# Scores ahead of the query projection, norm logarithm ahead of the query squares, in a pipelined windowed-attention kernel

## The chip, the cores and the metric

One core of one Trainium2 chip runs the whole program. The metric is the time of one execution on the device, in microseconds (us). The core's engines work side by side and meet at semaphores: TensorE (PE in the rows, its weight loads PEld), VectorE (DVE), ScalarE (ACT), GpSimd (POOL) and SyncE (SP), which issues the transfers.

## What is computed

x is 8 sequences of 256 tokens of 128 numbers. After a layer norm one branch is a linear attention with a small convolution; the other is six layers, each a windowed attention and a gated feed-forward part. The result is x plus the first branch times silu of the second. Nearly all of the time goes to the six layers:

```python
def attn_layer(x, Wqkv, qs, ksc, Wo):
    q, k, v = split(x @ Wqkv)             # 16 heads of 64
    q = l2norm(q) * qs;  k = l2norm(k) * ksc
    q, k = rotary(q), rotary(k)
    out = local_attention(q, k, v)        # window 32: own window and the one before
    return out @ Wo

for i in range(6):
    x = attn_layer(shift_tokens(x), ...) + x
    x = ffn_layer(shift_tokens(x), ...) + x
```

## The kernel before

**Units and slots.** A layer of one sequence is a batch: 6 layers x 8 sequences are 48 batches, numbered n. A batch has four units u = 4n + j, j = 0 to 3: two groups of eight heads by two tiles of 128 tokens. The program is software-pipelined by hand. Each engine runs a loop over n, and its body writes out four slots, j = 0 to 3; a slot does the projections of unit u and later steps of older units. The order inside a slot is the order of the code, engine by engine, and engines wait for each other by counting semaphores. The first five batches and the last one are written out, the rest are loops with the same body.

**TensorE's slot** (body, L791): the query projection of unit u (project, L661: three matmuls of 512 columns, high and low parts of the numbers); the scores of unit u-3 (scores, L675: 64 matmuls of 64 columns into ps_s); the turned probabilities of u-4 (turn_p, L652); the key and value projections of u; q and k of u-2 turned into ps_s (turn_qk, L639); work of the feed-forward part and the output projection, which differs by slot; the values of u-4 (L701); at the end of slot 0 ln_spread (L741).

**ScalarE's slot** (body, L1066): copy of the attention output of u-5 (keep_attention, L1007), copy of v of u-1 (keep_v, L962), squares of the query projection of u (squares_of, L955), logarithm and exponential that give a first value of the norms of u-1 (start_norms, L1000), in slot 2 a square for the layer norm, the turned probabilities of u-4 (keep_p, L988: two copies), the exponential of the softmax of u-3 (L996), squares of the key projection, the copies of the turned q and k of u-2, the mask for the scores of u-2, which is copied into ps_s (lay_mask, L974), and in slots 1 to 3 two feed-forward copies. In slot 0 it ends with the table load for the gelu and the gelu itself; in slot 1 the table with logarithm and exponential is loaded again (load_exp, L1063), between the squares and start_norms.

**VectorE's slot** (body, L1373): steps of the layer norm and the feed-forward part in slots 1 to 3, the maximum and the shift of the softmax of u-3 (softmax_shift, L1298: row_max, then prob), the Newton steps of the norms of u-1 (newton, L1286: rn_a, rn_b, rnorm), the sums of the query squares of u (L1273), the rotary step on q of u (rotate, L1255: qk and qk_rot), the row sums of the softmax of u-3 (L1309), the rotary step on k, the sums of the key squares, and the clamp of the sums (L1278: ssq_c).

**GpSimd's slot** (body, L475): one of the gate of the feed-forward part (slot 1), the split of a slice of the next layer's weights (slot 2, not in the last layer) and the rounding of the next x (slot 3); then it multiplies q and k of u-1 with the norms, divides the probabilities of u-3 (L440) and adds the two halves of the rotary step of u.

**Who waits for whom, around the change.** The query projection of u waits for the rotary step on q of u-1, which frees ps_q; in slot 0 it also waits for the rounded x and the split weights. The scores of u-3 wait for q_turned, k_turned and mask_laid, which ScalarE gives at the end of the slot before. The squares of u wait for the query projection of u. start_norms of u-1 waits for the clamp of u-1, which is the last step of VectorE's slot before. The Newton step of u-1 waits for start_norms. The turning of q and k of u-2 waits for the softmax shift of u-3, since both use ps_s. The turned probabilities wait for the copy of the attention output of u-5.

Of the kernel before, what the change touches and what calls it, by code (L numbers as in the profile page):

```python
# [62 lines left out]
def build(nc, x, wq, wk, wv, wp, bp, conv_w, conv_b, wqkv, q_scale, k_scale, wo, ln_g, ln_b, w1, b1, w2,  # L63
          rotary, masks, eye, head_block, out):
    with ExitStack() as ctx:
# [9 lines left out]
        def sem(name):  # L75
            return ctx.enter_context(nc.semaphore(name))
# [77 lines left out]
        ps_q, ps_k, ps_qs, ps_tk = ps_qk[:, 0, :], ps_qk[:, 1, :], ps_s[:, 0, :], ps_s[:, 1, :]  # L154
# [3 lines left out]
        def scored(pair):  # L158
# [27 lines left out]
        q_done, k_done, v_done = sem("q_done"), sem("k_done"), sem("v_done")  # L186
# [10 lines left out]
        q_scaled, k_scaled, ssq_done, ssq_clamped, rn_step, rnorm_done = (  # L197
            sem(n) for n in ("q_scaled", "k_scaled", "ssq_done", "ssq_clamped", "rn_step", "rnorm_done"))
# [7 lines left out]
        def live(u):  # L206

            return not isinstance(u, int) or 0 <= u < UNITS * STEPS

        def live_batch(m):  # L210
            return not isinstance(m, int) or 0 <= m < STEPS

        def place(n, j, back):

            return n + (j - back) // UNITS, (j - back) % UNITS

        def wait(eng, s, value):

            if not isinstance(value, int) or value > 0:
                eng.wait_ge(s, value)  # L220
# [316 lines left out]
        def _(pe):  # L537
# [123 lines left out]
            def project(n, j, i, ps, free, done):  # L661

                u = UNITS * n + j
                octet, tile = j // 2, j % 2
                if j == 0 and i == 0:
                    pe.wait_ge(xs_ready, n + 1)
                    pe.wait_ge(w_split, n // BATCHES * SLICES + SLICES)
                wait(pe, free, u)
                toks = slice(P * tile, P * tile + P)
                cols = span(n // BATCHES % 2 * (3 * INNER) + i * INNER + octet * OCTET, OCTET)  # L670
                mm(ps[:], xs_hi[:, toks], w_hi[:, cols], True, False)
                mm(ps[:], xs_hi[:, toks], w_lo[:, cols], False, False)
                mm(ps[:], xs_lo[:, toks], w_hi[:, cols], False, True).then_inc(done, 1)

            def scores(u, j, s, pair=ps_s, laid=True):  # L675

                octet, tile = j // 2, j % 2
                pe.wait_ge(q_turned, u + 1)
                pe.wait_ge(k_turned, u + 1)
                if laid:  # L680
                    pe.wait_ge(mask_laid, u + 1)
                    nc.tensor.sem_inc(pe_passed, 1)
                else:
                    for head in range(2):
                        mm(pair[:, head, 0:OCTET // 2], ident_b[:], mask_b[:, tile, OCTET // 2 * head:OCTET // 2 * (head + 1)],
                           True, True)
                for g in range(4):
                    for odd in range(2):
                        w = 2 * (g % 2) + odd
                        for low in range(2):  # L690
                            c = 2 * (g // 2) + low
                            at = 64 * odd + WINDOW * low
                            for head in range(2):
                                rows = slice(64 * head, 64 * head + 64)
                                last = mm(pair[at:at + WINDOW, head, 64 * g:64 * g + 64],
                                          q_t[rows, s, P * c + WINDOW * w:P * c + WINDOW * w + WINDOW],
                                          k_t[rows, octet, c, WINDOW * (4 * tile + w):WINDOW * (4 * tile + w) + 64],
                                          False, True, skip_group_check=True)
                last.then_inc(s_done, 1)
# [91 lines left out]
            def body(n):  # L791
                for j in range(UNITS):
                    u = UNITS * n + j
                    project(n, j, 0, ps_q, q_scaled, q_done)
                    if live(u - 3):
                        scores(u - 3, (j - 3) % UNITS, (j - 3) % 2)
                    if live(u - 4):
                        turn_p(u - 4, j % 2)
                    project(n, j, 1, ps_k, k_scaled, k_done)
                    if isinstance(n, int) and u == 0:  # L800
                        bias_fold()
                    project(n, j, 2, ps_v, v_copied, v_done)
                    if live(u - 2):
                        turn_qk(u - 2, 0, j % 2)
                        turn_qk(u - 2, 1, j % 2)
                    if j == 0:
                        if live_batch(n - 5):
                            ff_down(n - 5)
                        if live_batch(n - 2):
                            out_projection(n - 2, 1)  # L810
                    if j == 1:
                        if live_batch(n - 2):
                            ln_mean(n - 2)
                        if live_batch(n - 3):
                            ff_up(n - 3, 0)
                    if j == 2:
                        if live_batch(n - 2):
                            ln_variance(n - 2)
                        if live_batch(n - 3):
                            ff_up(n - 3, 1)  # L820
                    if j == 3:
                        if live_batch(n - 3):
                            ff_up(n - 3, 2)
                        if live_batch(n - 1):
                            out_projection(n - 1, 0)
                    if live(u - 4):
                        values(u - 4, n - 1, j, j % 2)
                    if j == 0 and live_batch(n - 3):
                        ln_spread(n - 3, u, BATCHES + n - 4)
# [55 lines left out]
        def _(act):  # L885
# [69 lines left out]
            def squares_of(u, i, s):  # L955

                wait(act, ssq_done, 2 * (u - 2) + i + 1)
                act.wait_ge((q_done, k_done)[i], u + 1)
                nc.scalar.activation(squares[:, s, OCTET * i:OCTET * i + OCTET], (ps_q, ps_k)[i][:], ACT.Square  # L959
                                     ).then_inc((q_squared, k_squared)[i], 1)  # L960

            def keep_v(u, n, j):  # L962
                wait(act, o_done, u - 3)
                if j % 2 == 0:
                    wait(act, v_shifted[j + 1], 32 * n)
                act.wait_ge(v_done, u + 1)
                copy(v_own[:, j, :], ps_v[:]).then_inc(v_copied, 1)
# [32 lines left out]
            def start_norms(c, s):  # L1000

                act.wait_ge(ssq_clamped, c + 1)
                nc.scalar.activation(ssq_ln[:, s, :], ssq_c[:, s, :], ACT.Ln).then_inc(ssq_logged, 1)
                act.wait_ge(ssq_logged, c + 1)
                nc.scalar.activation(rn_0[:, s, :], ssq_ln[:, s, :], ACT.Exp, scale=-0.5).then_inc(rn_started, 1)
# [60 lines left out]
            def body(n):  # L1066
                for j in range(UNITS):
                    u = UNITS * n + j
                    if live(u - 5):
                        keep_attention(u - 5, *place(n, j, 5))  # L1070
                    if live(u - 1):
                        keep_v(u - 1, *place(n, j, 1))
                    squares_of(u, 0, j % 2)
                    if j == 1 and live_batch(n - 4):
                        load_exp()
                    if live(u - 1):
                        start_norms(u - 1, (j - 1) % 2)
                    if j == 2 and live_batch(n - 2):
                        ln_square(n - 2)
                    if live(u - 4):  # L1080
                        keep_p(u - 4, j % 2)
                    if live(u - 3):
                        softmax_exp(u - 3, (j - 3) % 2)
                    squares_of(u, 1, j % 2)
                    if live(u - 2):
                        keep_turned_q(u - 2, j % 2)
                        keep_turned_k(u - 2, (j - 2) % UNITS)
                        lay_mask(u - 2, j % 2)
                    if j >= 1 and live_batch(n - 3):
                        ff_copy(n - 3, j - 1)  # L1090
                    if j == 0 and live_batch(n - 4):
                        load_gelu()
                        gelu(n - 4)
                    if j >= 1 and isinstance(n, int) and n == LAST:
                        silu_start(j - 1)
# [421 lines left out]
```

## Time and profile before

| | us |
|---|---|
| median of 3 runs | 1680.26 |
| lowest, highest | 1675.05, 1681.73 |
| profiled execution, its own time | 1673.91 |
| its span | 1672.1 |

| engine | busy us | share of the span |
|---|---|---|
| TensorE matmul | 1592.4 | 95% |
| VectorE | 1474.8 | 88% |
| ScalarE | 1433.8 | 86% |
| GpSimd | 1314.5 | 79% |

The profile covers one execution. Its timeline rows are: start, duration, engine, line of the kernel, operation, what is written <- what is read, shape, count, and in brackets the idle time of the engine before it with what ended that. Matmuls overlap in the pipeline, so the start of the next one tells more than the end of one. Small VectorE and ScalarE operations overlap their neighbours by a tenth of a microsecond in the same way. The mean granted clock of TensorE over the execution is 0.987 of full speed.

### The profile page before, as it was taken

The page shows a single profiled execution, that of the slowest core. Times are in us where ns is not written, and L with a number is a line of the kernel's source. Part 1 is how long each engine was busy: PE and PEld are TensorE (multiplying, and loading weights), DVE is VectorE, ACT ScalarE, POOL GpSimd, SP SyncE. Part 2 cuts the span into 40 slices and gives each one's busy share as a digit, 9 for nine tenths or more (in the row PEclk, how much of TensorE's full clock was granted, in tenths as well). Part 3 has the DMA queues.
Part 4 walks back from the last instruction along what each step waited for, and adds up shares of the span by engine and source line. Part 5 has one row for each costly group of instructions (what it writes and reads, how often), then busy time and mean ns, then how long its engine had stood idle before and what let it go on. Part 6 is the DMA issues. An engine that isn't in the chain of part 4 may idle for free.

```text
span 1672.1 us, 69023 instructions
## 1 busy us (share of the span) xinstructions
PE 1592.4 (95%) x25972; PEld 1222.7 (73%) x25972; DVE 1474.8 (88%) x3011; ACT 1433.8 (86%) x2851; POOL 1314.5 (79%) x1305
## 2 busy tenths in 40 slices
PE   7779999999999999999999999999999999999995
PEld 5657777777777777777777777777777777777773
DVE  4499999999999999999999999999999999999974
ACT  4267998998899899889989989998998999999985
POOL 6088888888888888888878888887888878777865
PEclk9799999999999999999999999999999999999998
DMA  4111111111111111111111111111111101111000
GB/s 135 48 43 40 34 40 38 32 45 31 46 40 33 38 38 39 40 43 37 31 38 44 41 37 40 35 31 50 40 38 34 39 28 39 37 31 34 29 25 26
DMA packets 41426, 66.40 MB, mean 40 GB/s; under 512 B 7072, under 2 KB 16032, under 8 KB 41376
## 3 DMA queue, kind: packets, MB, share of 16 engines
q1 hardware_dynamic: 40224, 65.38, 13.1%
q8 instruction: 33, 0.54, 0.1%
q10 hardware_dynamic: 1152, 0.34, 0.1%
q14 instruction: 17, 0.14, 0.0%
HBM read 20.61 MB, written 1.05 MB: 13 GB/s over the span
## 4 chain that ended last, share of the span: by engine, by line
PE 58%; DVE 26%; issue 12%; ACT 3%; DVEq 1%; DMA 0%; POOL 0%; ACTq 0%; POOLq 0%
PE ps_s L539 13%; PE ps_a L539 11%; PE ps_qk L539 10%; PE ps_f L539 9%; PE ps_po L539 7%; DVE qk_rot L1269 5%; PE ps_v L539 4%; DVE qk L1267 4%; PE ps_po L658 4%; DVE ssq L1275 4%; DVE row_sum L1311 3%; DVE row_max L1302 3%; DVE prob L1305 2%; DVE xc L1324 1%; DVE rn_b L1292 1%
## 5 line engine op out<-in xcount | busy, mean ns | idle before, releaser
L436 POOL TENSOR_TENSOR qk<-qk,rnorm 128x512 f32<-128x512 f32 x384 | 393.4, 1046 | 142.7 <-DVE rnorm L1295 134.0
L428 POOL TENSOR_TENSOR qk<-qk,qk_rot 128x512 f32<-128x512 f32 x384 | 484.8, 1285 | 0.0
L443 POOL TENSOR_TENSOR prob<-prob,row_inv 128x512 f32<-128x512 f32 x192 | 200.7, 1045 | 115.5 <-DVE row_inv L1314 115.5
L1275 DVE TENSOR_REDUCE ssq<-squares 128x8 f32<-128x512 f32 x384 | 260.4, 678 | 3.4 <-ACT squares L959 3.4
L1267 DVE TENSOR_TENSOR qk<-ps_qk,table 128x512 f32<-128x512 f32 x384 | 262.2, 683 | 1.1
L1269 DVE TENSOR_TENSOR qk_rot<-ps_qk,table 128x512 f32<-128x512 f32 x384 | 260.7, 679 | 0.0
L959 ACT ACTIVATE squares<-ps_qk 128x512 f32<-128x512 f32 x384 | 232.3, 605 | 19.8 <-PE ps_qk L539 12.9
L953 ACT COPY p_bd<-ps_po 64x512 f32<-64x512 f32 x378 | 217.4, 575 | 20.9 <-PE ps_po L658 18.6
L539 PEld LDWEIGHTS ps_s<-ident,qk 128*128 128x128 f32 x1528 | 170.9, 140 | 77.2 <-DVE prob L1305 63.6
L539 PE MATMUL ps_s<-ident,qk 128*128 128x128 f32 x1528 | 202.9, 276 | 23.8 <-DVE prob L1305 22.9
L539 PE MATMUL ps_qk<-w_hi,xs_hi 128*128 (+1 forms) x384 | 189.1, 493 | 11.4 <-DVE qk_rot L1269 6.7
L539 PEld LDWEIGHTS ps_po<-p_bd,v_back 128*64 128x64 f32 x3056 | 162.2, 137 | 45.4 <-issue 31.4
L539 PE MATMUL ps_po<-p_bd,v_back 128*64 128x64 f32 x3056 | 192.9, 225 | 0.0
L539 PE MATMUL ps_po<-p_bd,v_own 128*64 128x64 f32 x3056 | 188.5, 222 | 0.0
L539 PE MATMUL ps_a<-attn_t,wo_sb 128*64 128x257 f32 x1536 | 185.8, 383 | 0.0
L1302 DVE TENSOR_REDUCE row_max<-ps_s 128x8 f32<-128x512 f32 x191 | 130.6, 684 | 62.5 <-PE ps_s L539 62.3
L539 PEld LDWEIGHTS ps_s<-k_t,q_t 64*32 64x32 f32 x12224 | 133.2, 105 | 70.3 <-issue 70.3
L953 ACT COPY attn_t<-ps_po 128x512 f32<-128x512 f32 x191 | 112.6, 589 | 64.8 <-PE ps_po L539 64.8
L539 PE MATMUL ps_s<-k_t,q_t 64*32 64x64 f32 x12224 | 164.1, 224 | 0.7 <-ACT ps_s L953 0.5
L539 PEld LDWEIGHTS ps_po<-p_bd,v_own 128*64 128x64 f32 x3056 | 155.2, 138 | 0.0
L539 PEld LDWEIGHTS ps_a<-attn_t,wo_sb 128*64 128x64 f32 x1536 | 105.7, 136 | 66.5 <-issue 17.6
L539 PE MATMUL ps_qk<-w_lo,xs_hi 128*128 (+1 forms) x384 | 152.7, 398 | 0.0
(207 smaller groups left out, 3516.9 us busy)
## 6 DMA issues: line engine op xcount, KB each, us to landing
v_back<-v_own SPq DMA_DIRECT2D x192, 192.0 KB, 2.4
w_raw<-in_wqkv SPq DMA_DIRECT2D x48, 192.0 KB, 2.4
v_back<-v_own SPq DMA_DIRECT2D x96, 64.0 KB, 2.1
wo_sb<-in_wo SPq DMA_DIRECT2D x12, 256.0 KB, 3.0
w_sb<-in_w SPq DMA_DIRECT2D x6, 341.0 KB, 3.1
w_sb<-in_w SPq DMA_DIRECT2D x6, 192.0 KB, 2.5
x_in<-in_x SPq DMA_DIRECT2D x4, 256.0 KB, 4.8
out<-s_out SPq DMA_DIRECT2D x8, 128.0 KB, 1.9
```

Source lines behind the costliest of these rows:

```text
L428: nc.gpsimd.tensor_tensor(qk[:, s, i, :], qk[:, s, i, :], qk_rot[:, s, i, :], ALU.add).then_inc(added, 1)
L436: nc.gpsimd.tensor_tensor(heads(qk[:, s, i, :]), heads(qk[:, s, i, :]), rnorm[:, s, 8 * i:8 * i + 8].unsqueeze(2).to_broadcast([P, 8, HEAD ...
L443: nc.gpsimd.tensor_tensor(heads(prob[:, s, :]), heads(prob[:, s, :]), row_inv[:, s, :].unsqueeze(2).to_broadcast([P, 8, HEAD]), ALU.mult). ...
L539: return nc.tensor.matmul(o, lhs, rhs, start=start, stop=stop, **kw)
L658: last = nc.tensor.transpose(ps[:, P * c:P * c + P], prob[:, s, P * c:P * c + P], ident[:])
L953: return nc.scalar.copy(o, i)
L959: nc.scalar.activation(squares[:, s, OCTET * i:OCTET * i + OCTET], (ps_q, ps_k)[i][:], ACT.Square).then_inc((q_squared, k_squared)[i], 1)
L1267: V.tensor_tensor(heads(qk[:, s, i, :]), heads(ps[:]), cos.unsqueeze(1).to_broadcast([P, 8, HEAD]), ALU.mult)
L1269: V.tensor_tensor(halves(qk_rot[:, s, i, :]), halves(ps[:])[:, :, ::-1, :], sin.rearrange("p (a c) -> p a c", a=2).unsqueeze(1).to_broadca ...
L1275: V.tensor_reduce(ssq[:, s, 8 * i:8 * i + 8], heads(squares[:, s, OCTET * i:OCTET * i + OCTET]), AX, ALU.add).then_inc(ssq_done, 1)
L1302: V.tensor_reduce(most, score, AX, ALU.max).then_inc(max_done, 1)
L1311: V.tensor_reduce(row_sum[:, s, :], heads(prob[:, s, :]), AX, ALU.add).then_inc(sum_done, 1)
```

## The change

Two lines move. In TensorE's body the scores of unit u-3 come first in each slot and the query projection of unit u follows. In ScalarE's body start_norms (logarithm and exponential) comes ahead of the query squares in slots 0, 2 and 3; in slot 1, where the table is loaded between the two, it stays behind.

```diff
@@ -791,9 +791,9 @@
             def body(n):
                 for j in range(UNITS):
                     u = UNITS * n + j
-                    project(n, j, 0, ps_q, q_scaled, q_done)
                     if live(u - 3):
                         scores(u - 3, (j - 3) % UNITS, (j - 3) % 2)
+                    project(n, j, 0, ps_q, q_scaled, q_done)
                     if live(u - 4):
                         turn_p(u - 4, j % 2)
                     project(n, j, 1, ps_k, k_scaled, k_done)
@@ -1070,10 +1070,12 @@
                         keep_attention(u - 5, *place(n, j, 5))
                     if live(u - 1):
                         keep_v(u - 1, *place(n, j, 1))
+                    if j != 1 and live(u - 1):
+                        start_norms(u - 1, (j - 1) % 2)
                     squares_of(u, 0, j % 2)
                     if j == 1 and live_batch(n - 4):
                         load_exp()
-                    if live(u - 1):
+                    if j == 1 and live(u - 1):
                         start_norms(u - 1, (j - 1) % 2)
                     if j == 2 and live_batch(n - 2):
                         ln_square(n - 2)
```

## Rows read from the trace of the kernel before

**Rows 1.** Windows by slot, batch 23: busy time and count of each engine.
```profile
core 0: us, PE busy (x) PEld busy (x) DVE busy (x) ACT busy (x) POOL busy (x), PEclk, DMA share, GB/s
806.17:815.32 9.15, 9.15 (x150) 7.04 (x150) 8.01 (x17) 8.31 (x15) 6.95 (x7) 1.00 0.17 50
815.32:822.23 6.91, 6.91 (x126) 5.57 (x124) 5.68 (x13) 6.50 (x13) 5.16 (x6) 1.00 0.10 28
822.23:829.48 7.25, 7.23 (x130) 5.59 (x126) 7.11 (x14) 7.07 (x16) 6.84 (x7) 1.00 0.12 36
829.48:838.65 9.17, 8.53 (x140) 6.16 (x138) 8.96 (x20) 7.41 (x18) 7.76 (x9) 1.00 0.07 21
sum 32.48, PE 31.81 PEld 24.37 DVE 29.77 ACT 29.29 POOL 26.71; mean PE 7.95 PEld 6.09 DVE 7.44 ACT 7.32 POOL 6.68
```

**Rows 2.** The same windows for batch 42, in the last layer: their sum.
```profile
sum 31.70, PE 31.57 PEld 24.41 DVE 28.99 ACT 29.16 POOL 25.17; mean PE 7.89 PEld 6.10 DVE 7.25 ACT 7.29 POOL 6.29
```

**Rows 3.** Waits from 200 to 1370 us: who for whom, us, times, longest.
```profile
PEld ps_s L539 <- DVE prob L1305: 51.5, 72, 1.0
DVE row_max L1302 <- PE ps_s L539: 51.2, 72, 0.8
```

**Rows 4.** Timeline, TensorE, head of slot 1: start, us, operation [idle before].
```profile
815.32 0.48 PE L539 MATMUL ps_qk<-w_hi,xs_hi 128*128 x1
...
816.20 0.86 PE L539 MATMUL ps_s<-k_t,q_t 64*32 64x64 f32 x64
816.99 0.66 PE L658 MATMUL ps_po<-ident,prob 128*128 128x128 f32 x4
```

**Rows 5.** Timeline, ScalarE, slot 1.
```profile
816.31 0.60 ACT L959 ACTIVATE squares<-ps_qk 128x512 f32<-128x512 f32 x1 [0.21 <-PE ps_qk L539]
...
818.47 0.22 ACT L1005 ACTIVATE rn<-ssq_ln 128x18 f32<-128x18 f32 x1
```

**Rows 6.** Timeline, VectorE, slot 1.
```profile
817.17 0.69 DVE L1302 TENSOR_REDUCE row_max<-ps_s 128x8 f32<-128x512 f32 x1 [0.82 <-PE ps_s L539]
817.99 0.69 DVE L1305 TENSOR_TENSOR prob<-ps_s,row_max 128x512 f32<-128x512 f32 x1
818.72 0.18 DVE L1289 SCALAR_TENSOR_TENSOR rn_a<-ssq_c,rn 128x18 f32<-128x18 f32 x1
```

**Rows 7.** Timeline, TensorE and VectorE, the turning in slots 2 and 3.
```profile
825.64 0.40 PE L539 MATMUL ps_v<-w_hi,xs_lo 128*128 x1
826.06 0.66 PE L539 MATMUL ps_s<-ident,qk 128*128 128x128 f32 x4
...
833.02 0.69 DVE L1305 TENSOR_TENSOR prob<-ps_s,row_max 128x512 f32<-128x512 f32 x1
833.77 1.09 PE L539 MATMUL ps_s<-ident,qk 128*128 128x128 f32 x8 [0.54 <-DVE prob L1305]
```

**Rows 8.** Timeline, VectorE and TensorE, slot 3 of batch 42.
```profile
1447.50 0.69 DVE L1305 TENSOR_TENSOR prob<-ps_s,row_max 128x512 f32<-128x512 f32 x1
1448.33 1.04 PE L539 MATMUL ps_s<-ident,qk 128*128 128x128 f32 x8
```

**Rows 9.** Timeline, ScalarE's mask in slot 1, TensorE's head of slot 2.
```profile
822.08 0.59 ACT L953 CAST ps_s<-mask_b 128x512 f32<-128x512 bf16 x1
822.23 0.50 PE L539 MATMUL ps_qk<-w_hi,xs_hi 128*128 x1
```

**Rows 10.** Timeline, ScalarE's waits in slot 0 (first row) and slot 3.
```profile
806.11 0.59 ACT L953 COPY attn_t<-ps_po 128x512 f32<-128x512 f32 x1 [1.01 <-PE ps_po L539]
...
832.37 0.22 ACT L1003 ACTIVATE ssq_ln<-ssq_c 128x18 f32<-128x18 f32 x1 [0.58 <-DVE ssq_c L1280]
```

**Rows 11.** A window of the prologue; timeline, one shape at two clocks.
```profile
50.00:60.00 10.00, 6.08 (x42) 4.96 (x42) 5.22 (x10) 4.00 (x7) 0.00 (x0) 1.00 0.01 3
...
1639.76 1.91 PE L539 MATMUL ps_s<-xn,w_sb 128*128 128x256 f32 x4
1655.91 1.03 PE L539 MATMUL ps_s<-xn,w_sb 128*128 128x256 f32 x4
```

## The prediction

> **What bounds the kernel now.** I read the windows by slot first. The span is a pipeline of 48 batches of four slots; from batch 4 on a batch repeats with a period of 32.48 us [rows 1] and, in the last layer, of 31.70 us [rows 2]. The 1170 us that the waits of rows 3 cover hold 36 long periods (a wait that comes twice a batch is counted 72 times there), and the last layer has 8 batches: 44 batches on which a change in the loop acts. In rows 1 TensorE is busy 9.15 of 9.15, 6.91 of 6.91, 7.23 of 7.25 and 8.53 of 9.17 us in slots 0 to 3. VectorE is the fuller one where TensorE isn't: 7.11 of 7.25 and 8.96 of 9.17 us in slots 2 and 3. So neither engine alone is the bound; the bound runs back and forth.
>
> Next the waits [rows 3]. TensorE waits for VectorE's softmax shift (DVE prob) twice a batch, and VectorE waits for the scores (PE ps_s) twice a batch. The timelines place them. In slot 1 TensorE starts the query projection at 815.32, the scores at 816.20, and the next step at 816.99 [rows 4]. ScalarE waits 0.21 us for that projection, then does squares, table load and logarithm, and the exponential starts at 818.47 and takes 0.22 [rows 5]. VectorE waits for the scores until 817.17, starts the shift at 817.99 and the first Newton step at 818.72 [rows 6]. The shift ends at 818.68 and the exponential at 818.69: two paths that both start at the head of slot 1 arrive within 0.01 us, and this is what the forecast turns on. From there VectorE runs on to the shift of slot 3, which ends at 833.71, and TensorE's turning of q and k starts at 833.77 after 0.54 us of idling [rows 7]. Then TensorE has hardly a gap until the head of the next slot 1. The cycle is: TensorE from slot 3 through slot 0 to the head of slot 1; query projection and scores; VectorE through slots 1, 2 and 3; TensorE again. In the last layer the turning of slot 3 starts at 1448.33, after a shift that starts at 1447.50 and ends at 1448.19 [rows 8]: there TensorE itself is last, by about 0.1 us.
>
> **The scores go first.** No instruction is added or removed on TensorE: 64 score matmuls and 3 projection matmuls trade places, as long together as before. The scores come one projection sooner, 816.20 - 815.32 = 0.88 us, and the projection comes one score block later, 816.99 - 816.20 = 0.79 us [rows 4]. What this does in each slot:
>
> Slot 0: VectorE may start its maximum up to 0.88 us sooner. TensorE is full here and doesn't wait for VectorE, so the gain ends in idle time. ScalarE's squares come 0.79 later; behind them it waited for the turned probabilities anyway. Cost: zero, and the cover is TensorE's own queue.
>
> Slot 1, where ScalarE's order isn't changed: the squares start when the later projection is done, 816.31 + 0.79 = 817.10. Queued behind them on ScalarE are the table load, the logarithm and the exponential, which VectorE's Newton step waits for. It starts at 818.72 + 0.79 = 819.51. The shift, for its part, is over 0.88 us sooner, near 817.8, so VectorE stands idle for 1.7 us and everything behind the Newton step is 0.79 late: the sooner scores are worth nothing, because the other of the two equal paths has grown.
>
> Slot 2: the scores now stand at the head, and they need the mask that ScalarE lays at 822.08 to 822.67 in slot 1, while TensorE is free at 822.23 [rows 9]. Until now the query projection filled that time. ScalarE has no wait in which to recover from the head of slot 1 on, so the mask is down at 822.67 + 0.79 = 823.46, the scores start near 823.50, and TensorE idles 1.27 us. From the head of the slot to the turning TensorE took 826.06 - 822.23 = 3.83 us; the last projection before it starts at 825.64 and leaves room after 0.23, at 825.87 [rows 7], so 0.19 of it is waiting and 3.64 is work. It turns at 823.50 + 3.64 = 827.14, 1.08 us late. VectorE is 0.79 late and no longer last.
>
> Slot 3: TensorE was free at 833.77 - 0.54 = 833.23 [rows 7] and is now free at 834.31; VectorE's shift ends at 833.71 + 0.79 = 834.50. VectorE is last, the slot is 0.79 late, and that goes once around the cycle. In the last layer TensorE is last, so the 1.08 of slot 2 stays.
>
> **The norm logarithm goes ahead of the squares** in slots 0, 2 and 3. It is two instructions of 0.22 us [rows 5], the same number as before. In slot 3 ScalarE waited 0.58 us for VectorE's clamped sums after the squares were done [rows 10]; now the squares stand behind that wait, so their start-to-start time of 0.5 us is no longer hidden in it and ScalarE's later work is another 0.5 late, 1.3 in all. It has 1.01 us of waiting before its first copy of the next slot 0 [rows 10], and TensorE's 0.79 on top: 1.3 fits into 1.8. Slot 0 has cover too; in slot 2 the clamped sums are due when ScalarE comes to them, to within 0.1. Cost zero, gain zero: in these slots VectorE never waits for the exponential.
>
> No DMA is issued in another place, SyncE's and GpSimd's queues keep their order, and GpSimd's work follows VectorE's.
>
> **Sum.** 36 x 0.79 = 28.4 us, 8 x 1.08 = 8.6 us, together 37.0 us against the profiled execution's own 1673.9, or 1710.9. That execution is 6.3 us under the median of the runs shown, 1680.3, and a little under their lowest; the sum is added to the median: 1717.3, given as 1717. What the trace doesn't show is how fast a score block starts behind values, and a projection behind scores. The nearest rows: a neighbour pair costs 0.88 for three projection matmuls against 0.79 for the scores [rows 4], so a seam may be worth 0.1 either way, and the four seams of a batch 0.4 either way; 44 x 0.4 = 18 us. I take zero, since each kind of block is still preceded by another one, and keep 18 us on both sides: 1699 to 1735.
>
> **Rivals.** (1) Faster: the sooner scores do pull VectorE ahead. For it: VectorE's two waits for scores are its only regular ones [rows 3]. It would need the Newton step of slot 1 to start before 818.72, that is a table load that isn't held by the squares; against it stand 0.21 us of waiting right ahead of those squares [rows 5]. Then the late mask of slot 2 costs 822.70 - 822.23 = 0.47 less the 0.19 waited there before, 0.28, and the 0.54 waited in slot 3 comes off at best: 36 x 0.54 - 8 x 0.28 = 17 us, 1663.
>
> (2) No change: the change doesn't do what it says. The scores stand first but wait for the mask, the projection waits behind them, and the log's move ahead gives ScalarE back what the squares lose. Some 0.1 us a batch either way, 1676 to 1684.
>
> (3) ScalarE becomes the bound. It is already without a wait from slot 1 to slot 3. If its lateness in slot 3 goes past the 1.8 us worked out above (1.3 by my reckoning), the mask of slot 3 holds the scores at the head of slot 0, and TensorE has nothing to catch up with. With 0.5 us more a batch: 44 x 0.5 = 22 on top, 1739.
>
> (4) TensorE's clock falls in the new 1.27 us gap. The granted clock stays at 1.00 (2.4 GHz) in all four slots with the present gap [rows 1], and even in a stretch in which TensorE was busy 6.08 of 10 us [rows 11]. Where it did fall, four matmuls of 256 columns took 1.91 instead of 1.03 us [rows 11]; 0.85 of some 7 us of one slot is 6 us a batch, 44 x 6 = 264, 1981.
> The Trainium skill (TensorE: Matmul & The Clock Gate, Part 1: The HAM clock gate) says that the clock is not a fixed one: the half rate is the default, and it is the engine's recent activity that releases it. By that rule a change that opens a gap in every batch could cost this; the rows above show no fall after longer pauses of work than this one, and nothing in the forecast rests on the rule.
>
> **How the numbers follow.** Forecast 0.72, faster 0.09, no change 0.10, ScalarE as the bound 0.08, clock 0.01. The likeliest case gives 1717. The range must leave out no more than 0.2: the faster and the no-change case are left out below and the clock above, ScalarE's is taken in, which gives 1694 (5 us of spread between runs below 1699) to 1743. A measurement of this kernel can tell 0.5%, 8.4 us, from no change. Faster by more 0.09, within 0.10, slower 0.81.
>
> **What the profile after would show.** Right: rn_a of slot 1 starts straight behind the exponential, with 1 us or more of VectorE idling; ScalarE waits about 1 us for the query projection ahead of the squares of slot 1, in place of 0.21; TensorE idles about 1.3 us at the head of slot 2, until ScalarE's mask; VectorE's waits for scores are gone or short; the period is 33.3 us (32.8 in the last layer). Wrong: if the first Newton step of slot 1 doesn't come later against the head of the slot, or if ScalarE has a wait somewhere in slots 1 and 2, the sum has no ground; a period of 32.0 us or less would be rival 1, one of 33.8 or more rival 3.

## The result and the profile after

The changed kernel takes 1721.2 us (median of 4 runs, 1717.5 to 1726.4) against 1677.7 us of the kernel before in runs beside it (1673.5 to 1681.7): a ratio of 1.0267, 95% interval 1.0238 to 1.0296. The forecast was slower, 1717 us, 1694 to 1743. The profiled execution has a span of 1720.3 us, 48.2 more than before.

The page's line of busy times, then the window of one long batch, from the head of slot 1 to the head of the next slot 1, which answers to the sum in [rows 1]:

```profile
PE 1573.0 (91%) x25972; PEld 1252.4 (73%) x25972; DVE 1452.7 (84%) x3011; ACT 1437.9 (84%) x2851; POOL 1314.1 (76%) x1305
...
801.22:834.65 33.43, 31.27 (x535) 24.91 (x534) 29.36 (x62) 29.36 (x59) 26.70 (x27) 1.00 0.11 33
```

TensorE's share falls from 95 to 91%, with the same 25972 matmuls and a granted clock of 1.00 in the window. The batch takes 33.43 us where it took 32.48. In the last layer the table load of ScalarE in slot 1 comes once a batch. The pair below (start, duration) is 32.97 us apart, the longest of the six such distances there; their mean is 32.92, where the period was 31.70 [rows 2]:

```profile
1470.88 1.28 ACT L1064 ACT_TABLE_LOAD   x1
...
1503.85 1.28 ACT L1064 ACT_TABLE_LOAD   x1
```

The waits from 200 to 1400 us, which hold the long batches (who for whom, us in total, times, longest), to be held against [rows 3]:

```profile
DVE rn_a L1291 <- ACT rn L1005: 64.2, 36, 1.8
ACT squares L959 <- PE ps_qk L539: 60.4, 71, 1.2
PE ps_s L539 <- ACT ps_s L953: 56.1, 36, 1.6
DVE qk L1269 <- PE ps_s L539: 35.4, 36, 1.0
...
PEld ps_s L539 <- DVE prob L1307: 24.4, 36, 0.7
```

Three waits are new or much longer: VectorE's Newton step for ScalarE's exponential (36 times, 1.8 us each), ScalarE's squares for the query projection, and TensorE's scores for ScalarE's mask (36 times, 1.56 us). VectorE's 51.2 us of waiting for scores [rows 3] are gone from the list; in its place stands a wait of 0.98 us for the turned q in slot 0, where VectorE has time. TensorE's waits for the shift are left in one slot of four instead of two.

Slot 1 of one batch, TensorE, ScalarE and VectorE, against [rows 4 to 6]:

```profile
800.58 0.71 PE L539 MATMUL ps_f<-ident,rnorm 128*128 128x128 f32 x4
801.22 0.86 PE L539 MATMUL ps_s<-k_t,q_t 64*32 64x64 f32 x64
802.01 0.50 PE L539 MATMUL ps_qk<-w_hi,xs_hi 128*128 x1
802.80 0.60 PE L658 MATMUL ps_po<-ident,prob 128*128 128x128 f32 x4
...
803.00 0.60 ACT L959 ACTIVATE squares<-ps_qk 128x512 f32<-128x512 f32 x1 [1.18 <-PE ps_qk L539]
803.62 1.28 ACT L1064 ACT_TABLE_LOAD   x1
805.16 0.22 ACT L1005 ACTIVATE rn<-ssq_ln 128x18 f32<-128x18 f32 x1
...
802.93 0.69 DVE L1307 TENSOR_TENSOR prob<-ps_s,row_max 128x512 f32<-128x512 f32 x1
805.41 0.18 DVE L1291 SCALAR_TENSOR_TENSOR rn_a<-ssq_c,rn 128x18 f32<-128x18 f32 x1 [1.79 <-ACT rn L1005]
```

And the start of ln_spread in the kernel before:

```profile
814.85 0.71 PE L539 MATMUL ps_f<-ident,rnorm 128*128 128x128 f32 x4
```

Counted from the start of ln_spread, the shift starts at 2.35 where it started at 3.14, so the scores did bring it forward by 0.79. The squares start at 2.42 instead of 1.46, the exponential at 4.58 instead of 3.62, and the Newton step at 4.83 instead of 3.87: all three 0.96 later. VectorE's next step in the order of its code is the Newton step, so it idles until then. From the start of this Newton step to the start of the shift of slot 3 it takes 14.32 us (805.41 to 819.73) where it took 14.30 (818.72 to 833.02), in both kernels without a wait: the 0.96 us go through to slot 3, and the mask isn't on that way.

Slots 2 and 3 of the same batch, against [rows 7, 9, 10]: ScalarE's mask, TensorE's scores at the head of slot 2, the turning in slots 2 and 3, ScalarE's logarithm of slot 3 and its first copy of slot 0.

```profile
808.77 0.59 ACT L953 CAST ps_s<-mask_b 128x512 f32<-128x512 bf16 x1
809.61 0.85 PE L539 MATMUL ps_s<-k_t,q_t 64*32 64x64 f32 x64 [1.55 <-ACT ps_s L953]
813.03 1.03 PE L539 MATMUL ps_s<-ident,qk 128*128 128x128 f32 x8
...
820.47 1.09 PE L539 MATMUL ps_s<-ident,qk 128*128 128x128 f32 x8 [0.24 <-DVE prob L1307]
819.07 0.22 ACT L1003 ACTIVATE ssq_ln<-ssq_c 128x18 f32<-128x18 f32 x1 [0.94 <-DVE ssq_c L1282]
825.29 0.59 ACT L953 COPY attn_t<-ps_po 128x512 f32<-128x512 f32 x1 [0.48 <-PE ps_po L539]
```

The turning of slot 2 stands 12.45 us behind ln_spread, against 826.06 - 814.85 = 11.21 before, so 1.24 late; that of slot 3 19.89 against 18.92, so 0.97 late, held by VectorE's shift. TensorE reaches it late in slot 2 and waits for VectorE in slot 3, as worked out.

### The profile page after: what moved, and what is told of

It is laid out like the page before. It is cut to its first block, busy times and chain, and to the rows that moved or that the text cites. A ratio compares the mean times of both kernels' runs of the same rounds, so it can differ in the third digit from the quotient of the medians.

```text
span 1720.3 us, 69023 instructions
## 1 busy us (share of the span) xinstructions
PE 1573.0 (91%) x25972; PEld 1252.4 (73%) x25972; DVE 1452.7 (84%) x3011; ACT 1437.9 (84%) x2851; POOL 1314.1 (76%) x1305
## 4 chain that ended last, share of the span: by engine, by line
PE 53%; DVE 26%; issue 12%; ACT 8%; DVEq 1%; DMA 0%; POOL 0%; ACTq 0%; POOLq 0%
PE ps_s L539 12%; PE ps_a L539 11%; PE ps_qk L539 9%; PE ps_f L539 9%; PE ps_po L539 6%; DVE qk_rot L1271 5%; DVE qk L1269 4%; DVE ssq L1277 4%; PE ps_v L539 3%; DVE row_sum L1313 3%; DVE row_max L1304 3%; ACT L1064 3%; DVE prob L1307 2%; PE ps_po L658 2%; ACT squares L959 2%
## 5 line engine op out<-in xcount | busy, mean ns | idle before, releaser
L539 PEld LDWEIGHTS ps_s<-ident,qk 128*128 128x128 f32 x1528 | 175.1, 140 | 50.0 <-DVE prob L1307 29.6
L539 PE MATMUL ps_qk<-w_hi,xs_lo 128*128 (+1 forms) x384 | 152.5, 397 | 0.0
L539 PE MATMUL ps_f<-xn,w_sb 128*128 128x256 f32 (+1 forms) x556 | 147.5, 388 | 0.5 <-ACT qk_rot L1036 0.5
```

Source lines behind the costliest of these rows:

```text
L539: return nc.tensor.matmul(o, lhs, rhs, start=start, stop=stop, **kw)
```

## The experiments

Theory A is that of the forecast: the loss enters through slot 1, by query projection, squares, table load, logarithm, exponential and Newton step. Theory B, the rival: it is TensorE's idling at the heads of slots 2 and 3, where the scores wait for the mask. Each ratio is to the kernel before, in runs beside it (medians 1676.0 to 1677.4 us).

### Slot 1 alone taken back

```diff
+                    if j == 1:
+                        project(n, j, 0, ps_q, q_scaled, q_done)
                     if live(u - 3):
                         scores(u - 3, (j - 3) % UNITS, (j - 3) % 2)
-                    project(n, j, 0, ps_q, q_scaled, q_done)
+                    if j != 1:
+                        project(n, j, 0, ps_q, q_scaled, q_done)
```

> The changed kernel, but in slot 1 TensorE does the query projection ahead of the scores again. Theory A (the loss enters through slot 1: query projection, squares, table load, logarithm, exponential, Newton step): the 0.95 us a batch go; ScalarE's wait ahead of the squares of slot 1 is 0.2 us again, Newton starts behind the shift, period 32.5 us; in the last layer some 0.3 us a batch stay, since the scores of slot 2 still wait for the mask. Ratio to before 1.000 to 1.003, about 1680 us. Theory B (the loss is TensorE's idling at the head of slot 2, where the scores wait for the mask): the head of slot 2 still idles about 0.5 us of the 1.55 us, so about a third of the 44 us stays: 1692 us or more, ratio 1.009.

Measured: 1677.6 us, ratio 1.0003 (0.9985 to 1.0021). Its waits over the long batches:

```profile
ACT squares L962 <- PE ps_qk L539: 26.9, 72, 0.6
PE ps_s L539 <- ACT ps_s L956: 23.8, 37, 1.4
```

Its table loads in slot 1, from 190 to 1600 us (how many, duration in ns, start of the first and the last):

```profile
L1067 ACT ACT_TABLE_LOAD  x44: 1283/1283/1283, 201.8 to 1593.7; - x44
```

TensorE still waits some 0.65 us a batch for the mask, and the Newton step's wait isn't among the waits any more. The first and the last table load of the loop are 1391.9 us apart, against 1390.2 in the kernel before and 1433.1 in the changed one. In the long batches the loads are 32.47 us apart, as before, so there the mask's wait costs nothing. In the last layer, where TensorE is last, they are 31.97 apart and not 31.70: there it costs 0.27 us a batch, 2 us in all, as the expectation had it, and too little for the ratio to tell. With three of four slots changed and the log ahead, all but these 2 us of the loss are gone. That is theory A, and B's 1692 falls; what is true of B is confined to the last layer.

### Slot 1 alone changed

The kernel before, with `if j == 1` in place of `if j != 1` around the later projection, and ScalarE's order of before.

> The kernel before, but in slot 1 alone TensorE does the scores ahead of the query projection; ScalarE's order is that of before. Theory A: the whole loss is there, 44 x 0.96 = 42 us, 1720 us, ratio 1.025, with 1.8 us of VectorE's waiting ahead of the Newton step of slot 1. Theory B: the heads of slots 2 and 3 do not wait for a mask, so 1680 us, ratio 1.002 or less.

Measured: 1716.7 us, ratio 1.0239 (1.0209 to 1.0269).

```profile
DVE rn_a L1292 <- ACT rn L1008: 64.3, 36, 1.8
...
PE ps_s L539 <- ACT ps_s L956: 24.0, 36, 0.7
...
804.36 0.18 DVE L1292 SCALAR_TENSOR_TENSOR rn_a<-ssq_c,rn 128x18 f32<-128x18 f32 x1 [1.80 <-ACT rn L1008]
```

One slot of four gives the Newton step's wait to the tenth (64.3 against 64.2 us) and nearly the whole loss: 39 of 44 us by the medians, and 41.7 of the 42.9 us by which the stretch between the loop's first and last table load grows. The rest lies in the last layer, where the batch takes 32.66 us here and 32.92 in the changed kernel. The expectation for theory B had no mask wait here; there is one, of 0.67 us behind the projection in slot 2, since the mask itself is late. So this run alone doesn't clear the mask, but it shows where its lateness begins; the run ahead of it and the one without the mask's waits, below, clear it for the long batches.

### One part at a time

ScalarE's part alone (start_norms ahead in slots 0, 2 and 3, TensorE as before):

> Only ScalarE's part of the change: logarithm and exponential ahead of the squares in slots 0, 2 and 3, TensorE's order as before. Forecast of the sum: nothing, ratio 1.000, 0.998 to 1.002. In slot 3 ScalarE's later work comes some 0.5 us later and its wait ahead of the first copy of slot 0 is that much shorter. Rival: the 0.5 us reach the bound in each batch, 44 x 0.5 = 22 us, ratio 1.013.

Measured: 1676.7 us, ratio 0.9998 (0.9986 to 1.0011). The two waits that the sum spoke of, in the kernel before and in this one:

```profile
ACT attn_t L953 <- PE ps_po L539: 44.1, 72, 1.0
...
ACT ssq_ln L1003 <- DVE ssq_c L1280: 20.7, 36, 0.6
```
```profile
ACT ssq_ln L1003 <- DVE ssq_c L1282: 41.6, 71, 1.0
ACT attn_t L953 <- PE ps_po L539: 24.9, 72, 0.5
```

The wait for the clamped sums grows by 20.9 us and the wait ahead of the first copy shrinks by 19.2: the 0.5 us a batch moved from one cover into the other, as the sum had it.

TensorE's part alone (the scores ahead in all slots, ScalarE as before):

> Only TensorE's part of the change: scores ahead of the query projection in all four slots, ScalarE's order as before. Theory A (all of the loss comes through slot 1, where ScalarE's order is the same in both kernels): as slow as the changed kernel, ratio 1.024 to 1.028, about 1720 us; the logarithm's new place is worth nothing here too. Rival: the logarithm ahead of the squares makes up for part of the later squares in slots 0, 2 and 3, where without it the Newton step is held as well: then 1735 us or more.

Measured: 1716.7 us, ratio 1.0246 (1.0226 to 1.0265). Its Newton steps wait in a second slot too, and still it isn't slower:

```profile
DVE rn_a L1289 <- ACT rn L1005: 79.0, 70, 1.8
```

79.0 us in 70 waits against 64.2 in 36: 15 us of waiting more, at no cost in the long batches (33.37 us each, against 33.41 in the changed kernel), because it lies in slot 0, where VectorE has time. In the last layer the batch takes 33.20 us against 32.92, so there the log's new place is worth 0.28 us a batch, 2 us in all; in the long ones it costs 0.04. In sum the whole loss is TensorE's part, and the log's new place neither helps nor hurts with it by the time (the intervals of this and the changed kernel overlap).

### The path dosed without touching TensorE

```diff
+                    if j == 1 and live_batch(n - 4):
+                        act.wait_ge(q_done, u + 1)
+                        wait(act, extra_done, n - 4)
+                        nc.scalar.activation(extra[:], ps_q[:], ACT.Square).then_inc(extra_done, 1)
                     squares_of(u, 0, j % 2)
```

> The kernel before with one more ScalarE operation of 0.49 us (a second square of the same bank into a buffer that nobody reads) ahead of the squares of slot 1, in the 44 batches with a table load. It doses the path squares, table load, logarithm, exponential, Newton step without touching TensorE. Theory A: that path ties with the scores' path to within 0.01 us, so the dose comes out nearly whole: 44 x 0.48 = 21 us, 1698 us, ratio 1.0125. Theory B (ScalarE has room there and the loss of the change is TensorE's): less than 0.1 us a batch, ratio 1.002 or less.

Measured: 1702.7 us, ratio 1.0148 (1.0125 to 1.0170), or 25 us by the ratio, 21 to 28 by its interval. ScalarE's slot 1:

```profile
800.18 0.59 ACT L955 COPY v_own<-ps_v 128x512 f32<-128x512 f32 x1
801.06 0.60 ACT L1078 ACTIVATE extra<-ps_qk 128x512 f32<-128x512 f32 x1 [0.28 <-PE ps_qk L541]
801.55 0.59 ACT L961 ACTIVATE squares<-ps_qk 128x512 f32<-128x512 f32 x1
```

and the copy of v in slot 1 of the kernel before:

```profile
815.51 0.59 ACT L953 COPY v_own<-ps_v 128x512 f32<-128x512 f32 x1
```

From the copy of v to the first square it is 0.88 us, where it was 816.31 - 815.51 = 0.80 [rows 5], then 0.49 more for the extra one: the dose is 0.57, not 0.49, and 44 x 0.57 = 25.1 us. It comes out whole: a long batch takes 33.06 us in this trace where it took 32.47, 0.59 more. The path through the squares has no slack in the kernel before, as [rows 5, 6] said, and a delay on it is paid in full.

### The cure: the table load ahead of the squares as well

```diff
-                    if j != 1 and live(u - 1):
+                    if j == 1 and live_batch(n - 4):
+                        load_exp()
+                    if live(u - 1):
                         start_norms(u - 1, (j - 1) % 2)
                     squares_of(u, 0, j % 2)
-                    if j == 1 and live_batch(n - 4):
-                        load_exp()
-                    if j == 1 and live(u - 1):
-                        start_norms(u - 1, (j - 1) % 2)
```

> The changed kernel, and ScalarE also does the table load, the logarithm and the exponential ahead of the squares in slot 1, so that nothing which the Newton step waits for stands behind the query projection. Theory A: the loss goes, and the sooner scores are worth something for the first time; the Newton step starts behind the shift, about 0.8 us sooner against the head of slot 1 than in the kernel before, but the rotary step of slot 1 then waits for the turned q on TensorE, which leaves 0.2 us a batch: 36 x 0.2 = 7 us, 1670 us, ratio 0.996 (0.993 to 0.999). Theory B: the mask still comes behind the head of slot 2 and TensorE still idles there, 1700 us or more.

Measured: 1666.1 us, ratio 0.9927 (0.9906 to 0.9948). One table load's place turns a loss of 2.7% into a gain of 0.7%. VectorE in slot 1, ln_spread of this batch starting at 808.25:

```profile
810.60 0.69 DVE L1305 TENSOR_TENSOR prob<-ps_s,row_max 128x512 f32<-128x512 f32 x1
811.31 0.34 DVE L1289 SCALAR_TENSOR_TENSOR rn_a<-ssq_c,rn 128x18 f32<-128x18 f32 x1
...
813.07 0.69 DVE L1267 TENSOR_TENSOR qk<-ps_qk,table 128x512 f32<-128x512 f32 x1 [0.38 <-PE ps_s L539]
...
DVE qk L1267 <- PE ps_s L539: 48.5, 72, 1.0
PE ps_s L539 <- ACT ps_s L953: 23.1, 73, 1.3
```

The Newton step starts 3.06 behind ln_spread, 0.81 sooner than before, and the rotary step then waits 0.38 us for the turned q, as expected. The period is 32.23 us (TensorE's query projections of slot 0 at 800.52 and 832.75): 36 x 0.25 = 9 us. In the last layer the batch takes 31.81 us instead of 31.70, so that the whole stretch between the loop's first and last table load is 7.5 us shorter (1382.7 against 1390.2), which is what was expected. The medians differ by 11.3. In the trace the first table load stands at 197.3 us, 3.0 sooner than before, but it also stands 2.2 and 2.7 us sooner in the traces of the two parts of the change alone, which are not faster. So where the rest of the 11 us comes from stays open.

Now without the mask's waits at the heads of slots 2 and 3, where the projection is first again:

> As the kernel with the table load ahead of the squares in slot 1, but in slots 2 and 3 TensorE does the query projection first again, so that the scores there don't wait for the mask at the head (0.3 us of TensorE's idling in each of these slots). Theory A: these waits cost nothing in 36 of 44 batches, since VectorE is last in slots 2 and 3, held by the turned q of slot 1; in the last layer 0.3 us a batch come off: 2 to 3 us, 1664 us, ratio 0.992. Rival: the mask waits hold the cycle, 44 x 0.3 = 13 us come off, 1653 us.

Measured: 1667.4 us, ratio 0.9949 (0.9931 to 0.9967): no gain by the time, whose interval can't tell the 2 to 3 us expected. The same view of the table loads, in the kernel above and in this one:

```profile
L1064 ACT ACT_TABLE_LOAD  x44: 1283/1283/1283, 197.3 to 1580.0; - x44
L1067 ACT ACT_TABLE_LOAD  x44: 1283/1283/1283, 200.8 to 1580.9; - x44
```

The stretch is 2.6 us shorter, 1380.1 for 1382.7, and all of it comes off in the last layer (31.47 us a batch for 31.81). The long batches take 32.23 us in both. That is the clearest blow to theory B: in the 36 batches where VectorE is last its wait can be there or not. In the last layer, where TensorE is last, it costs 0.3 us a batch.

And, added to this last version, a step against the wait that does hold, the one for the turned q:

```diff
+                    if j != 1:
+                        project(n, j, 2, ps_v, v_copied, v_done)
                     if live(u - 2):
                         turn_qk(u - 2, 0, j % 2)
                         turn_qk(u - 2, 1, j % 2)
+                    if j == 1:
+                        project(n, j, 2, ps_v, v_copied, v_done)
```

> As the kernel with slots 0 and 1 swapped and the table load ahead, and in slot 1 TensorE turns q and k of the older unit ahead of the value projection (0.70 us sooner). VectorE's 0.38 us of waiting for the turned q in slot 1 is what holds the cycle now; it goes, and the shift of slot 3 comes that much sooner, until TensorE is last: 36 x 0.38 = 14 us off, 1651 us, ratio 0.984; in the last layer TensorE is last and nothing comes off. If the turned q doesn't hold the cycle, the time stays at that of the kernel without this step.

Measured: 1649.6 us, ratio 0.9846 (0.9829 to 0.9863), the best version here, 27 us under the kernel before.

```profile
805.99 1.03 PE L539 MATMUL ps_s<-ident,qk 128*128 128x128 f32 x8
806.78 0.48 PE L539 MATMUL ps_v<-w_hi,xs_hi 128*128 x1
...
805.68 0.35 DVE L1295 SCALAR_TENSOR_TENSOR rn_a<-ssq_c,rn 128x18 f32<-128x18 f32 x1
806.98 0.68 DVE L1273 TENSOR_TENSOR qk<-ps_qk,table 128x512 f32<-128x512 f32 x1
...
802.63:834.39 31.76, 31.38 (x537) 24.70 (x534) 29.52 (x62) 29.20 (x59) 26.71 (x27) 1.00 0.12 35
```

The turning now starts 3.36 us behind ln_spread (802.63) in place of 4.04 before, VectorE's rotary step follows its sums without a wait, and the batch takes 31.76 us, of which TensorE is busy 31.38. As long as TensorE's work takes these 31.38 us, another order has at most the other 0.4 us a batch to give.

### Is any of it the scores' place?

The table load ahead with TensorE's old order:

> TensorE's order as in the kernel before; on ScalarE, in slot 1 alone, table load, logarithm and exponential ahead of the squares. Theory A (two tied paths): the path through the squares gets 0.8 us shorter, but the path scores, maximum, shift is unchanged and takes over 0.1 us sooner: at most 44 x 0.1 = 4 us off, ratio 0.997 to 1.000. Rival (the logarithm alone is the bound of slot 1, and the gain of 10 us of the kernel that also has the scores first is owed to this step): 1667 us, ratio 0.993.

Measured: 1670.2 us, ratio 0.9965 (0.9950 to 0.9980). 6 us off where at most 4 were expected; the bound lies inside the interval. VectorE in slot 1:

```profile
815.04 0.69 DVE L1307 TENSOR_TENSOR prob<-ps_s,row_max 128x512 f32<-128x512 f32 x1
815.65 0.17 DVE L1291 SCALAR_TENSOR_TENSOR rn_a<-ssq_c,rn 128x18 f32<-128x18 f32 x1
```

The Newton step starts 0.61 us behind the start of the shift, where it started 0.73 behind it in the kernel before (817.99 to 818.72 [rows 6]). Freed of the exponential it overlaps the end of the shift. So the two paths of slot 1 were not equal to 0.01 us: the one through the squares was last, by 0.12. The long batch takes 32.34 us instead of 32.47, and 44 x 0.12 = 5.3 us is the gain.

The same with the turned q ahead too:

> As the kernel with the turned q and k ahead of the value projection in slot 1 and the table load ahead, but with the query projection ahead of the scores in all four slots, as in the kernel before. It asks what the sooner scores are worth in the best version (1650 us). Theory A: the shift path holds slot 1 again, so nearly all of the gain goes: 1672 us, ratio 0.996 (0.994 to 1.000). Rival: the turned q was the bound all along, and the scores' place is worth nothing: 1650 us, ratio 0.985.

Measured: 1680.7 us, ratio 1.0026 (1.0013 to 1.0038), a miss: neither 1672 nor 1650. TensorE in slot 1:

```profile
819.82 1.09 PE L539 MATMUL ps_s<-ident,qk 128*128 128x128 f32 x8 [0.41 <-DVE prob L1310]
820.67 0.48 PE L539 MATMUL ps_v<-w_hi,xs_hi 128*128 x1
```

The turning waits for the shift, which here ends at 819.76, so it idles 0.41 us in which the value projection used to run. I had asked only who waits for the moved step and not what it waits for. The step that is worth 18 us behind the sooner scores (1667.4 to 1649.6) costs 10 us without them (1670.2 to 1680.7); the traces show it too, with 32.56 us for a long batch instead of 32.34, and 31.96 instead of 31.58 in the last layer. So the sooner scores are worth 31 us (1680.7 to 1649.6) once the table load is out of the way and the turned q is ahead. The two kernels of this last comparison also differ in slot 0's order on TensorE and in the log's place in slots 0, 2 and 3, which no run took apart here; by itself the log's place was worth nothing.

## Why the prediction was right

**The tie in slot 1** held where the forecast needed it: the path through the squares had no slack. The dose of 0.57 us that came out as 25 us, and the loss that came and went with slot 1 alone, show it. The reading itself, two ends 0.01 us apart, was off: a small step of VectorE can start 0.08 us ahead of the end of the one before it (815.65 and 815.73), so the shift's path had 0.12 us of slack. The table load ahead in TensorE's old order showed it. Here, where it was the last path that grew, this made no difference.

**Slot 1's delay** was 0.79 in the sum and is 0.96. The mis-sized term is the seam: behind ln_spread the scores start 801.22 - 800.58 = 0.64 us later, where the projection started 815.32 - 814.85 = 0.47 later. The sum had put seams at up to 0.1 each and taken zero. TensorE's own slot isn't longer: from ln_spread to the turning of slot 1 it takes 4.06 us after and 4.04 before. What is lost ahead of the score block comes back behind it: the turned probabilities start 0.23 us behind the projection's last matmul (802.57 to 802.80), where the scores started 0.33 behind it (815.87 to 816.20), and the key projection follows the turned probabilities 0.05 us sooner. But the squares see only the part ahead of them.

**Slot 2**: an idle time of 1.27 was forecast and 1.55 is there; the turning was to be 1.08 late and is 1.24. The mask is down 0.96 late instead of 0.79, which is the same 0.17. Two more errors cancel by luck: the scores start 0.25 us behind the mask's end (809.36 to 809.61) where the sum had 0.04, and from them to the turning it is 3.42 us (809.61 to 813.03) where it had 3.64. **Slot 3**: VectorE last, 0.79 forecast, 0.97 measured. **ScalarE's cover**: its wait ahead of the first copy of slot 0 was to shrink by about 0.5 from 1.01 and is 0.48.

**The sum** was 37.0. The loop gives 36 x 0.95 and 7 x 1.22, 42.8 us: between the first and the last table load of the loop there are 1433.1 us where there were 1390.2. So 0.79 and 1.08, the two terms of the sum, were both some 0.15 too small. Of the 48.2 us of the two spans 1.9 lie ahead of that stretch, which is the lateness of the first load itself (0.96) and some 0.9 that I can't place, and 3.5 behind it. Of these, 2.1 lie between the last two table loads of the program, 14.49 us apart where they were 12.42; there the granted clock was 0.76 and 1.00. The change has no part in that: with TensorE's part of the change alone they are 12.42 apart at 1.00, with ScalarE's alone 14.59 at 0.77. The medians differ by 43.5. That the forecast of 1717 is only 4 us off is in part luck: the sum was 6.5 us short of the medians' difference, and it was added to a median of 1680.3 where the runs beside the result gave 1677.7.

**The log's move** cost and gave nothing, by its own run. **The rivals**: the clock stayed at 1.00 in the loop's windows with idle times of 1.55 us on TensorE in each batch; ScalarE didn't become the bound; "no change" and "faster" failed on slot 1. The faster rival named its condition rightly, a table load that isn't held by the squares: given that, the kernel is faster, though by 11 us and not by the 17 at best, since VectorE's rotary step then waits for the turned q.

## What to carry to other kernels

Where two paths into one instruction end together, to within 0.1 us here, making one shorter gives next to nothing and what the swap adds to the other is paid whole, in every turn of the loop. What a wait costs depends on who is last: the same wait for the mask cost nothing in 36 batches and 0.3 us a batch in the last layer, and a time with an interval of 0.2% didn't show it while the distance between two instructions of the loop did. Before swapping two blocks, list for each what is queued behind its consumer on the in-order engine; here it was a table load of 1.28 us, and it could go ahead of the instruction that waits. Ask of a moved step both who waits for it and what it waits for: the same move gave 18 us and cost 10, by whether what it waits for was done.

## What the runs showed of the hardware

A table load of ScalarE takes 1.28 us in all 46 cases of its line, 44 in slot 1 and two at the end. In slot 1 of the kernel before it stands between the squares, which end at 816.91 [rows 5], and the logarithm:

```profile
816.92 1.28 ACT L1064 ACT_TABLE_LOAD   x1
...
818.22 0.22 ACT L1003 ACTIVATE ssq_ln<-ssq_c 128x18 f32<-128x18 f32 x1
```

It starts 0.01 us behind the one and ends 0.02 us ahead of the other (818.20 to 818.22). The Trainium skill (ScalarE: Activation LUTs, What ACT_TABLE_LOAD costs) has the same load but adds a drain of 1.38 us for each switch to another set. The two differ: no such time shows on either side of the load here, and the measurement decides.

VectorE's last Newton step of slot 2 is 0.98 us long instead of 0.18 in the long batches, before and after alike. In the kernel before it ends when GpSimd's split of weights does, at 827.31 and 827.27:

```profile
826.27 1.00 POOL L416 TENSOR_TENSOR w_lo<-w_raw,w_hi  x1 [0.26 <-POOL w_hi L413]
826.33 0.98 DVE L1295 SCALAR_TENSOR_TENSOR rnorm<-rn_b,rn 128x18 f32<-128x18 f32 x1
```

In the last layer, where GpSimd has no split, the same step takes 0.18 (at 1441.61), and the period is 0.78 us shorter. The Trainium skill (SBUF — State Buffer, SBUF: two separate sides) says that VectorE and GpSimd share a pair of ports, and that an instruction which has it holds it until it ends. The rows agree, but no run here took the split away with all else left, so it isn't shown.
